# A decoder layer on one core: the last normalisation of the first half earlier, the first experts inside the attention rounds, routing products amid experts, and eight token products on GpSimd

## The reference

```
x = x + local_attention(layernorm(x))           # 8 heads, blocks of 12, 24 keys each, relative positions, tanh cap
x = x + cross_attention(layernorm(x), ctx)      # 16 heads of 64: q = ln(x) Wq, k, v = ln(ctx) Wkv, rotary k,
                                                # softmax(clip(q k / 8, -11, 11)) v, Wo, bo
x = x + mixture(layernorm(x)):                  # xf = layernorm(x), [1024 tokens, 128]
    a  = xf P_w^T
    dw1, dw2, dw3 = top-3 of 12 softmax weights of a U1^T, a U2^T, a U3^T     # dense [1024, 12], 9 zeros in each row
    h  = sum over e of (xf W1[e]^T) * dw1[:, e]     # 128 -> 512
    y  = sum over e of (gelu(h) W2[e]^T) * dw2[:, e] + dw3 b2
```

## Time and profile before

| | |
|---|---|
| median of 3 runs | 455.76 us (454.59 to 459.03) |
| the profiled execution | 457.88 us, its span 456.1 us |
| busy share of the span | PE 93%, DVE 75%, POOL 54%, ACT 43% |
| rounds of cross attention | about 62 to 301 us |
| first mixture | 304 to 386 us |
| second mixture | 386 to 456 us |

### The profile page before, as it was taken

The page is one execution under the profiler, slowest core; times in us unless marked ns, Lnnn a source line. Parts: engine busy times, 40 slices in busy tenths (PEclk is TensorE's granted clock), DMA queues, the critical chain, the costliest instruction groups (busy, mean ns, idle before and its releaser), DMA issues.

```text
span 456.1 us, 8468 instructions
## 1 busy us (share of the span) xinstructions
PE 422.6 (93%) x3168; PEld 310.3 (68%) x3168; DVE 340.6 (75%) x700; ACT 196.3 (43%) x312; POOL 244.4 (54%) x217
## 2 busy tenths in 40 slices
PE   3997789999999999998996998979989999999996
PEld 2666666666766766666764676748767788888885
DVE  8788658979997577987665688797985993654554
ACT  7758363664555353554234544423546543200000
POOL 5757248996898768885963664563432442000000
PEclk9999999999999999999997999989999999999999
DMA  7675414000000000000000000424627660000000
GB/s 181 170 162 82 88 23 79 0 1 1 0 2 1 1 1 1 0 1 2 0 2 1 1 1 0 142 47 69 140 46 191 118 133 1 6 6 11 8 6 13
DMA packets 75434, 19.85 MB, mean 44 GB/s; under 512 B 66741, under 2 KB 73834, under 8 KB 75394
## 3 DMA queue, kind: packets, MB, share of 16 engines
q1 hardware_dynamic: 72628, 18.27, 18.9%
q10 hardware_dynamic: 2766, 1.04, 1.0%
HBM read 17.27 MB, written 2.02 MB: 42 GB/s over the span
## 4 chain that ended last, share of the span: by engine, by line
PE 71%; DVE 12%; SPq 5%; issue 5%; ACT 4%; POOL 2%; DMA 1%; DVEq 0%; ACTq 0%; POOLq 0%
PE psum L1162 11%; PE psum L1145 9%; PE psum L955 8%; PE psum L1343 5%; PE psum L1344 5%; PE psum L1342 5%; PE psum L1306 4%; PE psum L1308 4%; PE psum L1307 4%; PE psum L1181 3%; SPq L375 3%; PE psum L1172 3%; PE psum L1064 3%; ACT e_sb L781 2%; DVE rden L1566 1%
## 5 line engine op out<-in xcount | busy, mean ns | idle before, releaser
L528 POOL TENSOR_TENSOR e_part<-e_sb 128x512 f32<-128x512 f32 x64 | 88.8, 1403 | 49.6 <-DVE e_sb L1559 37.6
L781 ACT ACTIVATE e_sb<-psum 128x1024 f32<-128x1024 f32 x64 | 62.2, 1022 | 20.9 <-PE psum L1145 20.9
L1162 PE MATMUL psum<-e_sb,v_sb 128*64 128x256 f32 x512 | 64.0, 391 | 0.8 <-ACT v_sb L688 0.8
L1145 PE MATMUL psum<-q_t,kT 64*128 64x256 f32 x512 | 64.2, 389 | 0.0
L1761 DVE SCALAR_TENSOR_TENSOR x_sb<-psum,dw,x_sb 128x128 f32<-128x128 f32 x96 | 33.7, 351 | 36.9 <-PE psum L1344 34.3
L1559 DVE TENSOR_SCALAR e_sb<-e_sb 128x1024 f32<-128x1024 f32 x64 | 54.7, 888 | 5.4 <-ACT e_sb L781 5.3
L1566 DVE RECIPROCAL rden<-psum 128x256 f32<-128x256 f32 x32 | 55.8, 1744 | 0.3
L760 ACT ACTIVATE kT<-psum 128x512 f32<-128x512 f32 x32 | 19.1, 598 | 85.6 <-PE psum L1064 85.3
L1145 PEld LDWEIGHTS psum<-q_t,kT 64*128 64x128 f32 x512 | 46.7, 186 | 9.6 <-issue 5.0
L568 POOL TENSOR_TENSOR xeT_lo<-xeT,xeT_hi 128x512 fp32r<-128x512 f32 x24 | 30.8, 1289 | 40.5 <-ACT xeT_hi L795 38.0
L520 POOL TENSOR_TENSOR k_rot<-rope_a,rope_b 128x512 f32<-128x512 f32 x32 | 42.2, 1319 | 18.5 <-DVE rope_b L1446 18.5
(11 more groups left out here) (194 smaller groups left out, 773.6 us busy)
## 6 DMA issues: line engine op xcount, KB each, us to landing
w_raw<-in_L_ffn_W_dram SPq DMA_DIRECT2D x96, 64.0 KB, 2.3
gates<-gate_dram SPq DMA_DIRECT2D x6, 768.0 KB, 4.4
ctx_sb<-in_ctx_dram SPq DMA_DIRECT2D x4, 256.0 KB, 6.1
vbd<-v_dram SPq DMA_DIRECT2D x16, 52.6 KB
v_dram<-v_tok SPq DMA_DIRECT2D x4, 136.0 KB, 3.6
raw<-in_L_xattn_Wkv_dram SPq DMA_DIRECT2D x2, 256.0 KB, 5.2
k_rot<-in_L_xattn_Wkv_dram SPq DMA_DIRECT2D x2, 256.0 KB, 4.4
k_rot<-in_L_xattn_Wq_dram SPq DMA_DIRECT2D x2, 256.0 KB, 5.6
```

The source lines that it names most:

```text
L528: pool.tensor_tensor(e_part[:, p % 2, half, :, :], e_sb[:, i % ERING, :, 0, :], e_sb[:, i % ERING, :, 1, :], ALU.add)\
L781: act.activation(e_sb[:, i % ERING, :, :, :].rearrange("p a k t -> p (a k t)"), psum[:, a:a + 2, :].rearrange("p a b -> p (a b)"), ACT.Exp ...
L1145: mm = pe.matmul(psum[:, 2 * (i % 2) + a, t * S:(t + 1) * S], kT[rows, p % 3, kt * P:(kt + 1) * P], q_t[rows, j % 2, p % 2, :], start=True ...
L1162: mm = pe.matmul(psum[DX * a:DX * a + DX, pv_bank(p), 0:S], v_sb[g % 2][:, kt, 2 * pp + a, :], e_sb[:, i % ERING, a, t, :], start=(kt == 0 ...
```

## The change

Four edits, all of order; no product is added or removed.

1. In round 22 POOL makes `rstd` of half 0 ahead of the sums of weights; DVE makes `nm` right behind the clips; ACT normalises ahead of `keys_turned`.
2. `spread_weights` for experts 0 and 1 goes into PE's rounds 29 and 30, both into bank 5 (`gate_bank`); DVE's `expert_tokens(0)` and `turn_weights(0)` go to the end of round 29, `weights_lo(0)`, `turn_weights(1)` and `expert_tokens(1)` to the end of round 30; ACT's and POOL's parts of expert 0's tokens go to round 29. The last `sum_weights` goes behind expert 0, the last `divide` behind expert 2's tokens on DVE, and the last projection behind expert 1.
3. The routing of half 1 begins one expert later, and three of its stages, "tokens", "scores" and "turn", are issued amid an expert, behind its second chunk; so is the first spread of half 1. The last normalisation of half 1 is one expert later.
4. `expert_tokens` of experts 4, 6, 8 and 10 of each half is made by POOL (`pool_tokens`); `tokens_made` waits for the two counters.

The diff, cut to what moves work:

```diff
+        def gate_bank(n):
+            return 5 if n < 2 else 5 - n % 2
...
-        ROUTE_2 = {"tokens": 4, "address": 5, "scores": 6, "chosen": 7, "softmax": 8, "turn": 9}
+        ROUTE_2 = {"tokens": 5, "address": 6, "scores": 6, "chosen": 7, "softmax": 8, "turn": 9}
+        ROUTE_MID = {5: "tokens", 6: "scores", 9: "turn"}
+        POOL_TOKENS = tuple(range(4, NE, 2)) + tuple(range(NE + 4, 2 * NE, 2))
+
+        def tokens_made(queue, n):
+            by_pool = sum(m in POOL_TOKENS for m in range(n + 1))
+            queue.wait_ge(s["xe_done"], n + 1 - by_pool)
+            if by_pool:
+                queue.wait_ge(s["xe_pool_done"], by_pool)
...  # POOL
+                if r == NORM_ROUND:
+                    rstd_of(LN_F, NT // 2)
                 if r + 1 < NPAIR:
                     weights_summed(2 * r + 2)
                     weights_summed(2 * r + 3)
                     halves_summed(r + 1)
-                if r == NORM_ROUND:
-                    rstd_of(LN_F, NT // 2)
                 if r in ROUND_KEYS:
                     key_sum(r + K_LEAD)
+                if r == NPAIR - 3:
+                    token_rest(0)
...
+            def pool_tokens(n):
+                half, e = divmod(n, NE)
+                g = GLOADS.index((half, e // GE))
+                pool.wait_ge(s["xeT_lo_done"], n - 1)
+                pool.wait_ge(s[f"ld_gate{g % 2}"], 16 * (g // 2 + 1))
+                pool.tensor_tensor(xeT[:, n % 2, :], gates[:, g % 2, e % GE, :], xnT[:, half, :], ALU.mult).then_inc(s["xe_pool_done"], 1)
+            for n in range(1, 2 * NE):
                 token_rest(n)
-                if n == 2:
+                if n == 4:
                     rstd_of(LN_F + NT // 2, NT // 2)
+                if n + 2 in POOL_TOKENS:
+                    pool_tokens(n + 2)
...  # ACT
                 route_1(2 * r)
+                if r == NORM_ROUND:
+                    final_normalize(0)
...
                 if r + 3 < NPAIR:
                     keys_turned(r + 3)
                 route_1(2 * r + 1)
-                if r == NORM_ROUND:
-                    final_normalize(0)
+                if r == NPAIR - 3:
+                    tokens_hi(0)
...
                 if r == NPAIR - 1:
-                    tokens_hi(0)
-            tokens_hi(1)
+                    tokens_hi(1)
...  # PE
+                if r in (NPAIR - 3, NPAIR - 2):
+                    spread_weights(r - NPAIR + 3)
...
-                sum_weights(r)
+                if r < NPAIR - 1:
+                    sum_weights(r)
...
-                if r == NPAIR - 2:
-                    spread_weights(0)
-            spread_weights(1)
...
+                    if c == 1 and beside == "spread":
+                        spread_weights(NE)
+                    elif c == 1 and beside:
+                        route(1, beside, 7)
...
-                first_mixture(n)
+                first_mixture(n, "spread" if n + 2 == NE else ROUTE_MID.get(n))
                 if n == 0:
+                    sum_weights(NPAIR - 1)
+                if n == 1:
                     for t in range(TPB):
                         mm = project(B - 1, t, psum[:, 7, t * D:(t + 1) * D])
```

More of the change, by code:

```diff
@@ L437, in load_gates @@
                     before, last = GLOADS[g - 2]
-                    sp.wait_ge(s["xe_done"], before * NE + (last + 1) * GE)
+                    tokens_made(sp, before * NE + (last + 1) * GE - 1)
                 rows = gate_dram[half, q * GE:(q + 1) * GE].rearrange("e t -> (e t)")
@@ L596, in _ @@
                     pool.tensor_copy(spread[:, :, :], pick[:, 0:GE, None].to_broadcast([SPLIT, GE, P])).then_inc(s["spread_done"], 1)
-            for n in range(2 * NE):
+            def pool_tokens(n):
[5 more added lines that the diff above has]
+            for n in range(1, 2 * NE):
                 token_rest(n)
-                if n == 2:
+                if n == 4:
                     rstd_of(LN_F + NT // 2, NT // 2)
+                if n + 2 in POOL_TOKENS:
+                    pool_tokens(n + 2)
         @block.scalar
@@ L790, in tokens_hi @@
             def tokens_hi(n):
-                act.wait_ge(s["xe_done"], n + 1)
+                tokens_made(act, n)
                 if n >= 3:
@@ L888, in _ @@
                     tokens_hi(n + 2)
+                if n == 4:
+                    final_normalize(1)
                 if n in BIAS and BIAS[n][0] == "turn":
@@ L1206, in spread_weights @@
                     pe.wait_ge(s["gate_src_done"], 1)
-                elif n == 1:
-                    pe.wait_ge(s["ox_done"], NPAIR - 1)
-                else:
-                    pe.wait_ge(s["xe_done"], n - 1)
-                pe.matmul(bank(5 - n % 2), spread[:, e, :], dw1T[:, :], start=True, stop=True).then_inc(s["spread_ps"], 1)
+                elif n < 3:
+                    tokens_made(pe, n - 1)
+                else:
+                    tokens_made(pe, n - 2)
+                pe.matmul(bank(gate_bank(n)), spread[:, e, :], dw1T[:, :], start=True, stop=True).then_inc(s["spread_ps"], 1)
             def route(half, stage, at):
@@ L1288, in _, with first_mixture @@
                 route_1(2 * r + 1)
-                if r == NPAIR - 2:
-                    spread_weights(0)
-            spread_weights(1)
-            def first_mixture(n):
+            def first_mixture(n, beside=None):
                 half, e = divmod(n, NE)
@@ L1347, in _ @@
             for n in range(2 * NE):
-                if n < 2 * NE - 2:
+                if n < 2 * NE - 2 and n + 2 != NE:
                     spread_weights(n + 2)
@@ L1352, in _ @@
                 for stage in ROUTE_2:
-                    if ROUTE_2[stage] == n:
+                    if ROUTE_2[stage] == n and ROUTE_MID.get(n) != stage:
                         route(1, stage, 7)
-                first_mixture(n)
+                first_mixture(n, "spread" if n + 2 == NE else ROUTE_MID.get(n))
                 if n == 0:
+                    sum_weights(NPAIR - 1)
+                if n == 1:
                     for t in range(TPB):
@@ L1359, in _ @@
                     mm.then_inc(s["tail_ps"], 1)
-            pe.wait_ge(s["xe_done"], 2 * NE)
+            tokens_made(pe, 2 * NE - 1)
             pe.wait_ge(s["wt_lo_done"], 2 * NE)
@@ L1600, in expert_tokens @@
                     dve.wait_ge(s["spread_ps"], half * GE + e + 1)
-                    gate = bank(5 - n % 2)
+                    gate = bank(gate_bank(n))
                 else:
@@ L1692, in _ @@
                     final_norm(0, 0)
-                if r == NPAIR - 1:
-                    weights_lo(0)
-                    turn_weights(1)
-                    dve.wait_ge(s["misc_ps"], MISC_NO["keys", NPAIR - 1] + 1)
-                    expert_tokens(0)
                 for b, rounds in LATENT_ROUNDS.items():
@@ L1703, in _ @@
                     clip(2 * r + 3)
+                if r == NORM_ROUND:
+                    final_norm(0, 1)
                 if r in CONTEXT_ROUND:
@@ L1716, in _ @@
                     key_unit(ROUND_KEYS[r])
-                if r == NORM_ROUND:
-                    final_norm(0, 1)
                 route_1(2 * r + 1)
+                if r == NPAIR - 3:
+                    dve.wait_ge(s["misc_ps"], MISC_NO["keys", NPAIR - 1] + 1)
+                    expert_tokens(0)
+                    turn_weights(0)
                 if r == NPAIR - 2:
-                    turn_weights(0)
-            divide(NPAIR - 1)
-            expert_tokens(1)
+                    weights_lo(0)
+                    turn_weights(1)
+                    expert_tokens(1)
             for n in range(2 * NE):
-                if n == 3:
-                    final_norm(1, 1)
-                if n < 2 * NE - 2:
+                by_dve = n < 2 * NE - 2 and n + 2 not in POOL_TOKENS
+                if by_dve and n + 2 != NE:
                     expert_tokens(n + 2)
@@ L1733, in _ @@
                     turn_weights(n + 2)
-                if n == 1:
+                if by_dve and n + 2 == NE:
+                    expert_tokens(n + 2)
+                if n == 4:
+                    final_norm(1, 1)
+                if n == 0:
+                    divide(NPAIR - 1)
+                if n == 2:
                     dve.wait_ge(s["tail_ps"], 1)
```

4 lines of the change are left out of this document (1 added, 3 removed).

## The result

The changed kernel takes **453.96 us** (median of 20 runs, 452.47 to 455.18); the kernel before, on the same chip, 456.48 (20 runs, 454.59 to 462.37). The ratio is 0.9947, 95% interval 0.9929 to 0.9965: faster by half a per cent, 2.4 us. I had forecast 447.2 us and a gain of 8.6. The profiled execution took 453.26 us, its span 451.3. That of before took 457.88, 1.4 us above its median, so a gain read from the two traces comes out somewhat larger than the one over all runs.

A forecast was written before the change was run, and what follows sets the result against it. PE, busy for 93% of the span, was taken as the bound, so only its idle or slow time could be won. 5.8 + 3.4 - 0.6 = 8.6 us off the 455.76 us median gave 447.2 us; low 444.3, high 451.6.

The forecast's parts named there:

- Part 1: Round 22, earlier normalisation of half 0: PE's v_sb wait falls from 5.42 to 1.2 us, low clock goes; gain 5.8 us.
- the two operations took from 237.36 to 238.72, 1.36 us, so they end near 233.9: Round 22: POOL's two operations for rstd, started when mv ends at 232.50, keep their old duration of 1.36 us.
- The lower clock falls away if 1.2 us is short enough: Round 23, after the v_sb wait: transposes and weigh_values products run at full clock again, worth 1.6 us.
- The clock stays low: Rival: idles near 239, 301 and 335 us keep the clock low; price 1.6 + 1.5 us at most; chance 0.17.
- the bound I had named: Round 22, upper bound 6.9 us: nm takes a third of its time, since POOL held it at 1.22 us.
- Part 2: End of the rounds, first experts moved into last rounds: 1.9 us of idle and 1.5 of clock; gain 3.4 us.
- The cover of 0.2 us for the last division: End of the rounds: last division ends near 307.5, the projection behind expert 1 needs it at 307.7; lateness paid one for one.
- Part 3: Final normalisation of half 1, from expert 3 to 4, transposes to the middle of 5: cover 0.4 us; taken at nothing.
- Part 4: Routing products amid experts: dw wait falls to about 0.65 us, a gate_src wait of 1.3 us arises; net -0.6 us.
- Part 5: Every second token product by POOL, eight of twenty-four: DVE relieved of 0.7 to 1.25 us each; gain nothing.
- Neither was late behind 342 us, so nothing: Behind 342 us: DVE and POOL were not late, so moving token products to POOL gains nothing.
- The port rival: Routing of half 1: four DVE operations each wait one POOL operation of 1.3 us; 452.4 us, half 449.8; chance 0.08.

The follow-up runs named there:

- e2: Changed kernel, with DVE making the offset nm ahead of its two clips in round 22 instead of behind them; 451.25 us, 0.9836 of the kernel before.
- p1b: Kernel before with only the earlier normalisation of half 0, and nm ahead of the clips; 449.53 us, 0.9826 of the kernel before.
- p1: Kernel before with only the earlier normalisation of half 0, nm behind the clips; 452.32 us, 0.9864 of the kernel before.
- g3: Part 1 in e2's order and Part 2 alone, routing of half 1 between whole experts, no POOL token products; 454.30 us, 0.9943 of the kernel before.
- f2: f1 with the bias transposes and products of both halves one expert later; 449.36 us, 0.9806 of the kernel before.
- f1: Changed kernel with step 16's token product made by DVE and nm ahead of round 22's clips; 449.66 us, 0.9835 of the kernel before.
- e3: Changed kernel with the bias transposes and product for half 0 issued amid expert 10; 453.88 us, 0.9918 of the kernel before.

## Why the prediction was wrong

**Part 1, forecast 5.8 us, got 3.3.** The step that failed is "the two operations took from 237.36 to 238.72, 1.36 us, so they end near 233.9". I carried POOL's duration to a place where DVE clips. On the trace's own clock they took from 230.87 to 233.12, 2.25 us, 0.9 us more. So the wait was 2.04 us where I had 1.2, and then "The lower clock falls away if 1.2 us is short enough" had no case: 1.6 us more. 0.8 + 1.6 makes 2.4 of the 2.5 us that are missing. At this place the rival "The clock stays low" came true, at the price it had. I had the rule before me and used it for `nm` and at part 5, not for POOL's two operations beside the clips. e2 and p1b show both: with this collision taken away part 1 is 6.1 us, the forecast and a little more (wait 0.77 us, since `nm` took 0.17 us; the bound I had named).

**Part 2, forecast 3.4 us, got 3.8.** Idle 0.75 us against 0.6, expert 0 in 2.95 us, the sum of weights at once, the projection without a wait. The cover of 0.2 us for the last division held. But 1.5 of the 3.8 us is the low clock of expert 0 in the trace of before, and that is chance: p1 has the same two waits (0.99 and 1.44 us) and ran expert 0 at full clock. So part 2 is worth 2.3 to 3.8 us by execution, and that the measured figure is so near the forecast is in part luck.

**Part 3, forecast nothing, got nothing** in the changed kernel; g3 shows that without it part 2 costs a wait of 1.85 us at `xeT_lo`.

**Part 4, forecast -0.6 us, got -1.1.** The wait for `gate_src` is 1.39 us against 1.3. `dw` is waited for 0.25 us against 0.65, but the expert ahead of it waits 0.31 us for `w1T_lo`. The waits make -0.6 us, as forecast; the other 0.5 us are in no bracket. About half of them stand at the wait for `w1T_lo`:

```profile
327.99 0.39 PE L1332 MATMUL psum<-xeT_hi,w1T_lo 128*128 128x512 f32 x1
328.69 0.47 PE L1330 MATMUL psum<-xeT_hi,w1T_hi 128*128 128x512 f32 x1 [0.31 <-DVE w1T_lo L1622]
329.00 0.40 PE L1331 MATMUL psum<-xeT_lo,w1T_hi 128*128 128x512 f32 x1
```

Unhindered products of this shape start 0.23 us apart; here it is 0.70 and 0.31, 0.55 us lost for a bracket of 0.31. The rest is open. As f2 shows, the wait for `gate_src` is a matter of how many PE rows lie between link and link: one expert later it is gone.

**Part 5, forecast 0, got -2.7 at one place.** The step that failed is "Neither was late behind 342 us, so nothing". It looks at waits of DVE and POOL and says nothing of the slack: the bias product had waited 0.46 us already, so the chain `h_lo`, `xeT`, `xeT_hi`, `dw3T` had no slack at all, and the 1.1 us more on DVE there were paid in full (1.08 us of waiting), and 1.6 us of low clock came on top. I had asked what POOL's work would do at stage "turn", where two-input operations are small, and not at the two largest ones. The port rival had the mechanism right and the place wrong: at "turn" the wait for `dw` came out shorter than forecast (0.25 us). I had also written that I should be wrong if a wait of over 2 us stood behind 235 us or the clock was low there; both came, 2.04 us and the two stretches of low clock.

The sum is 3.3 + 3.8 - 1.1 - 1.3 - 1.6 = 3.1 us (the fourth term is the 1.1 us of the `h_lo` pair and 0.2 us that I can't place). Taken without the two collisions (f1, with the 1.75 us of low clock at 258 set apart) the stretch is 222.4, 8.7 us less than before: the forecast's sum. That the two figures agree is partly luck: f1's low clock is set apart here and that of expert 0 in the trace of before is not. Over all runs f1 is 7.9 us below its runs of before by the medians, and p1b, which has part 1 alone in e2's order, is 8.0 us below the same runs. So over all runs only part 1 is shown, and the gain of part 2 rests on traces alone.

## What to carry to other kernels

A duration is read together with its neighbours: before moving a GpSimd operation, list which DVE operations will run beside it in the new order, and price the pair, not the operation. Of an engine that gets more work, ask not where it is waited for, but which waits of the bound engine are near zero or above through a queue it feeds: there, in this kernel, the price was one for one. And when a link of a chain is moved nearer, follow the chain to its last link (e3, f2, g1) and move the moved work's companions with it (g3). And before a wait is forecast to vanish with its low clock, ask whether another execution shows the same wait at full clock (p1 and p1b).
